# Four-layer transformer kernel: head unit 31's exponentials turned in two transfers, and new opening and order tables

## The chip, the cores and the metric

One core of a Trainium2 chip runs the whole program. Its engines have a queue of instructions each: PE (TensorE, matmuls, with its weight loads PEld), DVE (VectorE), ACT (ScalarE), POOL (GpSimd) and SP (SyncE, which here only issues DMAs). They run side by side and wait for one another by semaphores. The metric is the device time of one execution in microseconds; the number to predict is the median of several executions.

## The reference

The input is x, 1024 rows of 256. Four layers follow, each as `x = x + layernorm(f(layernorm(x)))`:

```python
qkv = (x @ w_qkv.T)                      # attention 0: 16 heads of 128, no mask
weights = softmax(q @ k.T / sqrt(128))
f0 = (weights @ v).reshape(...) @ w_out.T
hidden = silu(x @ wu.T) * (x @ wg.T)     # FFN 0: 1024 wide, ternary weights
f1 = hidden @ wd.T
scores = q_lat @ c_kv.T                  # attention 1: latent of 64, 16 heads of 16, causal
f2 = softmax(scores) @ c_kv @ v_eff
h = silu(x @ lut[gate_idx].T) * (x @ lut[up_idx].T)   # FFN 1: 688 wide, weights from a table of 16
f3 = h @ lut[down_idx].T
```

## The kernel before

**Splitting.** Products keep float32 accuracy although the operands are narrower: a value is split into an upper part (names that end in H or h) and a low part (L, l), and a product is three matmuls (lines 1000 to 1002). ACT makes the upper part from PSUM, DVE the low part.

**Stages.** `order_of_heads` (line 87) writes the order of attention 0 as a list of steps, `HEADS`. Each engine's program walks the same list and emits its own instructions of a step. FFN 0, attention 1 ("latent") and FFN 1 do the same with tables of short words (`order_of_ffn0`, `order_of_latent`, `order_of_ffn1`): a letter for the step, hexadecimal digits for its arguments. `m` is a row maximum, `w` a matmul of attention weights with its exponential, `c` the sum with the values, `u` and `h` the hidden layer of an FFN, `x` its split, `d` its down product, `s` the statistics of a layer norm, `o` and `i` its normalized outputs and inputs, `t` the transposes of the normalized input, `p` and `l` projections.

**Opening.** SP loads x in two halves and then the weights of heads 0 and 1; POOL issues the loads of two index tables (line 1946) ahead of all its work. PE runs 46 matmuls on a constant tile (`N_WARM`, line 1052). The strings `before` and `firsts` order what follows: statistics of x (`t`), normalized x (`n`), PE transposes (`T`) into XN's transposed halves xh and xl, the squares of the weights' columns (`k`, line 1381, ACT), their norm (`K`: PE, three small DVE instructions, then on POOL the scaling of both heads' weights wqr, line 1958, and q_unit, line 1966), the split of scaled weights (`Q`: wqh on ACT, wql on POOL, line 1972), and the projections `X` with their splits `x` (ACT) and `y` (DVE). `turn_in` and the projections share the two work banks 6 and 7.

**Head units.** 32 units follow, each half the queries of one head in four row blocks j. For a block: scores on PE (2 x 3 matmuls), `max` on DVE (L1661), exponential on ACT (L1423), 1/sum on DVE (L1671), normalized upper part to EP on ACT (`cast_e`, L1433), low part on DVE (`rest_e`, L1676). Then SP turns the block of EP, upper and low part together, with one transposing DMA into ET16 (L979), and `attend` (eight steps A0 to A7, three matmuls each) waits for all four blocks. `last` orders unit 31: behind the last `attend` of unit 30 stands a second run of 30 constant matmuls, then `attend` of unit 31 up to A4, the transposes of the next stage's input (`L7`), and A5 to A7.

```python
last = ("w3 i3 h3 L0 w4 l3 A7 W1 L1 L2 f0 L6 w5 L3 F0 A0 L4 A1 L5 A2 A3 A4 L7 A5 A6").split()
```

Of the kernel before, what the change touches and what calls it, by code (L numbers as in the profile page):

```python
# [30 lines left out]
N_WARM = (46, 30)  # L31
# [43 lines left out]
def f32(ap):  # L75
    return ap.bitcast(F32)
# [17 lines left out]
def order_of_heads():  # L94
# [13 lines left out]
    def project(what, *at):  # L108
# [4 lines left out]
    before = ("W0 t0 t1 n0 n1 n2 n3 k0 K0 n4 n5 n6 T0 Q0 v0 n7 T1 X0 x0 y0 Q1 X1 y1 X2 y2 x1 x2 x3 e0 v1 h0 S0 M0 "  # L113
             "v2 y3 e1 X3 x4 S1 i0 v3 M1 X4 S2 v4 e2 l0 M2 i1 i2 y4 x5 M3 S3 X5 y5 h2 l2 l1 h1 X6 X7 e3 y6 y7 "
             "x7 x6").split()
# [3 lines left out]
    for step in before:  # L119
# [7 lines left out]
        elif what == "k":  # L127
            todo.append(("square_wqk", j))
        elif what == "K":
            todo.append(("norm_wqk", j))  # L130
# [9 lines left out]
        else:  # L140
# [22 lines left out]
    weights = {(0, "w0"): [("norm_wv", 2)], (0, "w1"): [("scale_wv", 2), ("square_wqk", 2)],  # L163
               (0, "w2"): [("turn_norm", 2), ("split_wv", 2), ("norm_wqk", 2)],
# [3 lines left out]
    for u in range(NU + 1):  # L168
# [7 lines left out]
        for step in orders.get(u, order):  # L176
# [22 lines left out]
            for kind, ahead in weights.get((r, step), []):  # L199
                if h2 + ahead < H0:  # L200
                    todo.append((kind, h2 + ahead))
                    if kind in after and h2 + ahead + after[kind][1] < H0:
                        loads.append((after[kind][0], h2 + ahead + after[kind][1]))
# [70 lines left out]
def build(nc, a, out):  # L274
    with ExitStack() as top:
# [295 lines left out]
        for step in HEADS:  # L571
# [37 lines left out]
            elif what == "square_wqk":  # L609
                for i in range(4):  # L610
                    q_squared.mark(*at, i)
            elif what == "norm_wqk":
# [6 lines left out]
                for i in range(2):  # L619
                    q_back.mark(*at, i)  # L620
# [1559 lines left out]
```

## Time and profile before

| what | value |
|---|---|
| median of 3 runs | 897.76 us (896.94 to 898.62) |
| the profiled execution | 896.64 us, span 894.9 us |
| PE busy | 834.4 us, 93% of the span |
| DVE busy | 766.2 us, 86% |
| ACT busy | 607.9 us, 68% |
| POOL busy | 429.6 us, 48% |
| mean granted TensorE clock | 0.995 |

The span runs from the first to the last instruction; the execution is 1.7 us longer. The stages in time: opening 0 to about 30 us, head units to about 583, FFN 0 to about 646, latent attention to about 836, FFN 1 to the end. A timeline row gives the start, the busy time, the engine, the line, what is written and read, how many instructions it merges, and in brackets how long the engine sat idle before it and who released it.

### The profile page before, as it was taken

To read this page: it belongs to the slowest core of one execution; us is meant where nothing else is said; L and a number is where in the kernel's file an instruction comes from. 1 tells how busy PE (TensorE), PEld (TensorE's weight loads), DVE (VectorE), ACT (ScalarE), POOL (GpSimd) and SP (SyncE) were. 2 spreads that over 40 slices of the span, in tenths; PEclk is the share of its full clock that TensorE was granted. 3 is DMA by queue.
4 is the path that set the end of the run, shared out by engine and by line. 5 is a ranking of instruction groups with operands and counts; after the bars stand their busy time and mean duration, and the time that the engine had idled before them with its cause. 6 is when DMAs were issued, how large, how long until landed. Compare 5 with 4: busy or idle time off the path is not lost. (4 is left out here: it accounts for less than half of the span.)

```text
span 894.9 us, 13229 instructions
## 1 busy us (share of the span) xinstructions
PE 834.4 (93%) x4405; PEld 537.4 (60%) x4406; DVE 766.2 (86%) x1595; ACT 607.9 (68%) x1044; POOL 429.6 (48%) x456
## 2 busy tenths in 40 slices
PE   8889999999999989999998999989868999999997
PEld 3555665566566556566555666567754555554686
DVE  3788999899989999999999999766699796886647
ACT  5677767777788677776776777855565767758632
POOL 4134354444454448678679765142242354444301
PEclk9999999999999999999999999999989999999999
DMA  3487769958887677777766777630000000000001
GB/s 126 85 183 155 149 103 188 181 114 154 172 154 157 131 133 147 149 140 134 162 120 118 130 141 141 119 110 1 1 0 1 1 1 1 1 1 2 1 1 48
DMA packets 276868, 86.31 MB, mean 96 GB/s; under 512 B 267584, under 2 KB 272448, under 8 KB 276416
## 3 DMA queue, kind: packets, MB, share of 16 engines
q1 hardware_dynamic: 275520, 80.05, 45.9%
q0 software_dynamic: 992, 5.34, 2.2%
q8 instruction: 35, 0.57, 0.3%
q14 instruction: 33, 0.27, 0.1%
q10 hardware_dynamic: 288, 0.07, 0.0%
HBM read 17.29 MB, written 1.05 MB: 20 GB/s over the span
## 5 line engine op out<-in xcount | busy, mean ns | idle before, releaser
L1433 ACT ACTIVATE EP<-ps,rinv 128x1024 f16<-128x1024 f32 x128 | 142.3, 1113 | 46.7 <-DVE rinv L1671 42.9
L1676 DVE SCALAR_TENSOR_TENSOR EP<-ps,rinv,EP 128x1024 f16<-128x1024 f32 x128 | 163.3, 1276 | 3.8 <-ACT EP L1433 3.3
L1423 ACT ACTIVATE ps<-ps,nmax 128x1024 f32<-128x1024 f32 x128 | 139.2, 1088 | 34.8 <-DVE nmax L1661 34.3
L1661 DVE TENSOR_REDUCE nmax<-ps 128x1 f32<-128x1024 f32 x128 | 155.0, 1211 | 0.8 <-PE ps L1002 0.8
L1000 PE MATMUL ps<-KH,QH 128*128 128x512 f32 x256 | 115.3, 451 | 7.0 <-DVE KL L1643 4.2
L2018 POOL TENSOR_TENSOR wgu<-wgu,ptm 128x688 f32<-128x688 f32 x60 | 99.7, 1662 | 42.7 <-DVE ptm L1775 40.6
L1000 PE MATMUL ps<-ET,VH 128*128 128x512 f16 x256 | 97.2, 380 | 9.1 <-DMA ET<-EP 5.3
L2018 POOL TENSOR_TENSOR wdn<-wdn,ptm 128x512 f32<-128x512 f32 x45 | 57.7, 1283 | 92.0 <-DVE ptm L1775 90.8
L1002 PE MATMUL ps<-KH,QL 128*128 128x512 f32 x256 | 100.8, 394 | 0.0
L1001 PE MATMUL ps<-KL,QH 128*128 128x512 f32 x256 | 100.4, 392 | 0.0
L1002 PE MATMUL ps<-ET,VL 128*128 128x512 f16 x256 | 97.0, 379 | 0.0
L1001 PE MATMUL ps<-ET,VH 128*128 128x512 f16 x256 | 97.0, 379 | 0.0
L1531 ACT ACTIVATE ET<-ps 128x512 f32<-128x512 f32 (+3 forms) x144 | 60.6, 506 | 35.1 <-PE ps L1254 34.9
L1858 DVE CUSTOM_DVE_ANT_0 ps<-ps,tern 128x512 f32<-128x512 f32 (+3 forms) x128 | 72.1, 601 | 8.4 <-PE ps L1233 8.1
L1924 POOL TENSOR_TENSOR rs<-ve,mhalf 128x4 f32<-128x4 f32 (+2 forms) x22 | 19.3, 876 | 101.2 <-DVE ve L1580 78.8
L1000 PEld LDWEIGHTS ps<-KH,QH 128*128 128x128 f32 x256 | 48.2, 188 | 26.4 <-DVE EP L1676 6.9
L2080 POOL TENSOR_SCALAR_AFFINE_SELECT ET<-ET 128x128 f32<-128x128 f32 x96 | 28.4, 296 | 55.1 <-ACT ET L1531 49.6
L1002 PEld LDWEIGHTS ps<-KH,QL 128*128 128x128 f32 x256 | 48.0, 188 | 11.2
L1000 PE MATMUL ps<-xh,wqh 128*128 128x512 f16 x128 | 49.0, 383 | 4.4 <-DVE KL L1643 3.3
L1000 PEld LDWEIGHTS ps<-ET,VH 128*128 128x128 f16 x256 | 25.6, 100 | 45.2 <-DMA ET<-EP 8.6
L1001 PEld LDWEIGHTS ps<-KL,QH 128*128 128x128 f32 x256 | 48.3, 189 | 7.3
L1001 PE MATMUL ps<-xl,wqh 128*128 128x512 f16 x128 | 48.5, 379 | 0.0
(253 smaller groups left out, 2142.1 us busy)
## 6 DMA issues: line engine op xcount, KB each, us to landing
wqr<-in_wqk SPq DMA_DIRECT2D x16, 256.0 KB, 3.4
wgu<-in_tern POOLq DMA_DIRECT2D x3, 1024.0 KB, 6.7
wvr<-in_wv SPq DMA_DIRECT2D x8, 256.0 KB, 4.0
wor<-in_wo SPq DMA_DIRECT2D x16, 128.0 KB, 3.2
ET<-EP SPq DMA_TRANSPOSE x128, 4.3
X<-in_x SPq DMA_DIRECT2D x2, 512.0 KB, 5.7
prw<-in_down_idx POOLq DMA_DIRECT2D x2, 256.0 KB, 8.0
tern<-in_l_wuq_rep SPq DMA_DIRECT2D x1, 512.0 KB, 4.3
```

The source lines that it names most:

```text
L1000: e.matmul(dst, lh, rh, start=first, stop=False)
L1001: e.matmul(dst, lh, rl, start=False, stop=False)
L1002: return e.matmul(dst, ll, rh, start=False, stop=last)
L1423: e.activation(bank, bank, ACT.Exp, bias=nmax[:, c:c + 1], scale=1.0, accum_out=rsum[:, c:c + 1]).then_inc(exped.sem, 1)
L1433: e.mul(EP[:, n % NE_RING, 0, :], SB(u, j), rinv[:, c:c + 1]).then_inc(e_hi.sem, 1)
L1531: e.activation(ET[:, r, c:c + n1], ps[:, BANK[(*step, c)][0], n - n1:n], ACT.Exp).then_inc(weight_exped.sem, 1)
L1661: e.tensor_reduce(nmax[:, c:c + 1], SB(u, j), AX.X, ALU.max, negate=True).then_inc(maxed.sem, 1)
L1676: e.scalar_tensor_tensor(out=EP[:, n % NE_RING, 1, :], in0=SB(u, j), scalar=rinv[:, c:c + 1], in1=EP[:, n % NE_RING, 0, :], op0=ALU.mult, ...
L1858: e.tensor_tensor_reduce(src, src, mask[:, m0:m0 + n], 1.0, -3.0e38 if part == 0 else half, ALU.add, ALU.max, NM[:, p % 2, i8, col:col + 1 ...
L1924: e.tensor_tensor(rs[:, o, ts], ve[:, o, ts], mhalf[:, ts], ALU.pow).then_inc(ln_scale.sem, 1)
L2018: e.tensor_tensor(dst, dst, ptm[:, v % 2, 0:n], ALU.add).then_inc(lut_added.sem, 1)
L2080: e.affine_select(out=tile, in_=tile, compare_op=ALU.is_ge, fill=0.0, base=0, pattern=[[1, P]], channel_multiplier=-1).then_inc(masked.sem, 1)
```

## The change

- The last unit's `cast_e` and `rest_e` (unit 31) issue a transposing DMA each: the upper part once ACT has written it, the low part once DVE has. Both count on the block's semaphore, and `attend` waits for both. The other 31 units keep one transfer.
- Opening: x's second half is loaded behind the weights of heads 0 and 1; the two index loads become steps `I0`, `I1` further on; 24 constant matmuls instead of 46; squares, norm and scaling are done for head 0 alone and then for head 1 (`k0 K0 g0`, `k1 K1 g1`); the scaling on POOL is a step of its own (`scale_wqk`); the transposes of x go to banks 0 to 3; a new opening string.
- All three tables behind the heads are permuted: the same 83, 487 and 61 words.

```diff
-N_WARM = (46, 30)
+N_WARM = (24, 30)
...
-    before = ("W0 t0 t1 n0 n1 n2 n3 k0 K0 n4 n5 n6 T0 Q0 v0 n7 T1 X0 x0 y0 Q1 X1 y1 X2 y2 x1 x2 x3 e0 v1 h0 S0 M0 "
...
+    before = ("W0 k0 n0 t0 n1 g0 n2 Q0 K0 t1 n3 T0 v0 n5 n4 X0 n6 n7 y0 x0 T1 g1 x1 k1 x2 X1 X2 Q1 y1 K1 y2 x3 S0 "
...
     if what == "turn_in":
         for k in range(2):
-            take_work((*step, k), x_lo[at[0], k, at[1]])
+            if at[0] == 0:
+                BANK[(*step, k)] = (2 * at[1] + k, None)
+            else:
+                take_work((*step, k), x_lo[at[0], k, at[1]])
...
-            for i in range(2):
-                e.dma_start(X[:, 4 * i:4 * i + 4, :], x_v[:, 4 * i:4 * i + 4, :]).then_inc(x_in[i].sem, 16)
+            e.dma_start(X[:, 0:4, :], x_v[:, 0:4, :]).then_inc(x_in[0].sem, 16)
             for h in range(2):
                 e.dma_start(wqr[:, h, :, :], a["wqk"][:, h, :, :]).then_inc(wqk_in[h].sem, 16)
+            e.dma_start(X[:, 4:8, :], x_v[:, 4:8, :]).then_inc(x_in[1].sem, 16)
...
+                elif what == "cast_e" and at[0] == NU - 1:
+                    u, j = at
+                    w.wait_ge(*e_hi[u, j])
+                    w.wait_ge(*attended[u - 2, 7])
+                    e.dma_start(ET16[:, u % 2, 0:8, j * P:j * P + P], EP[:, (4 * u + j) % NE_RING, 0, :],
+                                transpose=True).then_inc(e_turned[(4 * u + j) % NE_RING].sem, 16)
+                elif what == "rest_e" and at[0] == NU - 1:
+                    u, j = at
+                    w.wait_ge(*e_lo[u, j])
+                    e.dma_start(ET16[:, u % 2, 8:16, j * P:j * P + P], EP[:, (4 * u + j) % NE_RING, 1, :],
+                                transpose=True).then_inc(e_turned[(4 * u + j) % NE_RING].sem, 16)
...
 # order_of_ffn0, first row of the table
-        s1044 V M h000 h010 x000 x010 o17 u020 u030 o15 h020 o16 o14 s1144 h030 x020 u040 h040 x030 i16 u050 D i15
+        s1044 V M h000 u020 h010 h020 x000 o14 o15 u030 x010 o17 o16 s1144 u040 h030 h040 x020 x030 u060 x040 i14
```

POOL at the program's start, before: rs and nb are the statistics of x, wqr the scaling of the query and key weights, wql their low part, wvs the squares of the value weights.

```order
9 L1946 DMA prw<-in_down_idx 128x512
10 L1946 DMA wgu<-in_down_idx 128x512
11 L1924 ISA
12 L1924 TENSOR_TENSOR rs<-ve,mhalf 128x4
13 L1929 TENSOR_TENSOR nb<-nm,rs 128x4
14 L1924 TENSOR_TENSOR rs<-ve,mhalf 128x4
15 L1929 TENSOR_TENSOR nb<-nm,rs 128x4
16 L1958 TENSOR_TENSOR wqr<-wqr,wfac 128x512 x2
17 L1966 TENSOR_SCALAR q_unit<-wpow 128x2 x2
18 L1972 TENSOR_TENSOR wql<-wqr,wqh 128x512
19 L1979 TENSOR_TENSOR wvs<-wvr 128x512
20 L1972 TENSOR_TENSOR wql<-wqr,wqh 128x512
```

And POOL there in the changed kernel:

```order
10 L1945 TENSOR_TENSOR rs<-ve,mhalf 128x4
11 L1950 TENSOR_TENSOR nb<-nm,rs 128x4
12 L1981 TENSOR_TENSOR wqr<-wqr,wfac 128x512
13 L1989 TENSOR_SCALAR q_unit<-wpow 128x1 x2
14 L1995 TENSOR_TENSOR wql<-wqr,wqh 128x512
15 L1945 TENSOR_TENSOR rs<-ve,mhalf 128x4
16 L1950 TENSOR_TENSOR nb<-nm,rs 128x4
17 L2002 TENSOR_TENSOR wvs<-wvr 128x512
18 L1981 TENSOR_TENSOR wqr<-wqr,wfac 128x512
19 L1989 TENSOR_SCALAR q_unit<-wpow 128x1 x2
20 L1995 TENSOR_TENSOR wql<-wqr,wqh 128x512
21 L1972 DMA prw<-in_down_idx 128x512
```

Head 0's scaling and split now stand ahead of the statistics of x's second half, and head 1's behind them.

PE at the start, in the changed kernel (before, 16 transposes stand together between the norm's matmul and the first projection, and 46 constant matmuls ahead of it):

```order
1 L1070 MATMUL ps<-filler 128x512 x24
2 L1115 MATMUL ps<-wsum,ones 128x2
3 L1030 MATMUL ps<-ident,XN 128x128 x8
4 L1018 MATMUL ps<-xh,wqh 128x512
5 L1019 MATMUL ps<-xl,wqh 128x512
6 L1020 MATMUL ps<-xh,wql 128x512
7 L1018 MATMUL ps<-xh,wqh 128x512
8 L1019 MATMUL ps<-xl,wqh 128x512
9 L1020 MATMUL ps<-xh,wql 128x512
10 L1030 MATMUL ps<-ident,XN 128x128 x8
```

The first projection, which needs only half 0 of x, has moved ahead of the second half's transposes.

DVE at the start of the latent stage, before: CS is the split latent, QH the first heads' keys, Q their queries, the ISA rows are row maxima.

```order
924 L1820 SCALAR_TENSOR_TENSOR CS<-ps,pat,R 128x512
925 L1575 BN_STATS st<-X 128x6 x2
926 L1578 BN_AGGR mv<-st 128x2 x2
927 L1580 TENSOR_SCALAR ve<-mv 128x2
928 L1586 TENSOR_SCALAR nm<-mv 128x2
929 L1596 TENSOR_TENSOR X<-X,XN 128x256 x2
930 L1840 TENSOR_TENSOR QH<-tern,R 64x512 x2
931 L1575 BN_STATS st<-X 128x6 x2
932 L1578 BN_AGGR mv<-st 128x2 x2
933 L1580 TENSOR_SCALAR ve<-mv 128x2
934 L1586 TENSOR_SCALAR nm<-mv 128x2
935 L1831 SCALAR_TENSOR_TENSOR Q<-ps,pat,R 128x512 x2
```

And in the changed kernel:

```order
926 L1605 TENSOR_SCALAR nm<-mv 128x2
927 L1841 SCALAR_TENSOR_TENSOR CS<-ps,pat,R 128x512
928 L1861 TENSOR_TENSOR QH<-tern,R 64x512 x2
929 L1615 TENSOR_TENSOR X<-X,XN 128x256 x2
930 L1852 SCALAR_TENSOR_TENSOR Q<-ps,pat,R 128x512
931 L1594 BN_STATS st<-X 128x6 x2
932 L1597 BN_AGGR mv<-st 128x2 x2
933 L1599 TENSOR_SCALAR ve<-mv 128x2
934 L1605 TENSOR_SCALAR nm<-mv 128x2
935 L1879 ISA ps,NM<-ps,tern 128x384
```

The first Q now stands ahead of the last statistics, and CS behind the statistics before it.

## Rows read from the trace of the kernel before

**Rows 1.** Busy time by stretch: start:end, length, each engine's busy time, clock, DMA.

```profile
core 0: us, PE busy (x) PEld busy (x) DVE busy (x) ACT busy (x) POOL busy (x), PEclk, DMA share, GB/s
400.00:500.00 100.00, 92.58 (x482) 59.44 (x483) 97.53 (x148) 69.38 (x106) 80.62 (x54) 1.00 0.72 132
...
590.00:626.00 36.00, 32.62 (x164) 24.51 (x163) 25.91 (x63) 21.95 (x41) 17.10 (x17) 1.00 0.21 68
...
660.00:700.00 40.00, 32.90 (x146) 20.98 (x146) 36.93 (x118) 21.78 (x39) 10.84 (x14) 0.99 0.00 1
700.00:750.00 50.00, 48.91 (x287) 29.52 (x285) 41.14 (x137) 36.25 (x82) 24.54 (x48) 1.00 0.00 1
```

**Rows 2.** Timeline of the opening, all engines: start, busy time, what.

```profile
1.39 11.93 PE L1052 MATMUL ps<-filler 128*128 128x512 bf16 x46 [1.39 <-POOL filler L1942]
...
8.29 2.07 ACT L1326 ACTIVATE XN<-X,nb,rs 128x256 f32<-128x256 f32 x4 [5.25 <-POOL nb L1929]
...
10.27 0.40 ACT L1381 ACTIVATE wsq<-wqr 128x256 f32<-128x256 f32 x1
...
10.83 1.02 POOL L1924 TENSOR_TENSOR rs<-ve,mhalf 128x4 f32<-128x4 f32 x1 [2.57 <-DVE ve L1580]
...
11.40 0.42 ACT L1381 ACTIVATE wsq<-wqr 128x256 f32<-128x256 f32 x1
...
13.15 0.28 PE L1096 MATMUL ps<-wsum,ones 128*128 128x4 f32 x2
...
14.12 2.04 POOL L1958 TENSOR_TENSOR wqr<-wqr,wfac 128x512 f32<-128x512 f32 x2 [1.99 <-DVE wfac L1703]
14.59 1.29 DVE L1604 SCALAR_TENSOR_TENSOR xl<-ps,xh 128x512 f16<-128x512 f32 x2 [0.55 <-ACT xh L1334]
...
16.76 1.16 POOL L1972 TENSOR_TENSOR wql<-wqr,wqh 128x512 f16<-128x512 f32 x1
...
18.11 0.39 PE L1000 MATMUL ps<-xh,wqh 128*128 128x512 f16 x1 [0.98 <-DVE xl L1604]
...
24.27 0.50 PE L1000 MATMUL ps<-KH,QH 128*128 128x512 f32 x1 [1.33 <-DVE KL L1643]
...
27.86 1.08 ACT L1423 ACTIVATE ps<-ps,nmax 128x1024 f32<-128x1024 f32 x1
```

**Rows 3.** DMAs: rate in 40 slices of 0:30; a load issued in 1.8:2.3, to landing.

```profile
GB/s 0 0 85 206 330 169 23 99 286 395 422 402 392 326 253 34 0 0 0 0 0 0 0 0 0 156 194 0 0 0 41 229 79 0 22 0 0 0 0 0
...
wqr<-in_wqk SPq DMA_DIRECT2D x1, 256.0 KB, 8.2
```

**Rows 4.** Timeline around the last head unit.

```profile
570.00 6.42 PE L1052 MATMUL ps<-filler 128*128 128x512 bf16 x29
577.16 0.38 PE L1000 MATMUL ps<-ET,VH 128*128 128x512 f16 x1 [0.74 <-DMA ET<-EP]
...
580.39 1.13 PE L1012 MATMUL ps<-ident,XN 128*128 128x128 f32 x8
...
578.62 2.08 ACT L1326 ACTIVATE XN<-X,nb,rs 128x256 f32<-128x256 f32 x4
```

**Rows 5.** Timeline, end of FFN 0 and start of the latent stage.

```profile
636.80 0.39 PE L1038 MATMUL ps<-KH,f0hh 128*128 128x256 f32 x1 [1.70 <-DVE XL L1607]
...
651.62 1.40 DVE L1840 TENSOR_TENSOR QH<-tern,R 64x512 fp32r<-64x512 f32 x2 [0.68 <-ACT tern L1522]
...
654.27 1.40 DVE L1831 SCALAR_TENSOR_TENSOR Q<-ps,pat,R 128x512 fp32r<-128x512 f32 x2
655.07 2.29 PE L1233 MATMUL ps<-QH,Q 128*128 128x256 f32 x7 [4.30 <-DVE Q L1831]
```

**Rows 6.** Busy time by stretch, the columns of rows 1: opening and latent start.

```profile
13.30:18.10 4.80, 2.37 (x19) 1.66 (x17) 2.53 (x7) 3.91 (x8) 3.82 (x6) 1.00 0.00 0
653.00:655.00 2.00, 0.00 (x0) 0.00 (x0) 1.90 (x9) 1.47 (x3) 1.14 (x2) 0.66 0.00 0
655.00:657.00 2.00, 1.93 (x7) 1.68 (x7) 1.99 (x9) 1.59 (x3) 1.70 (x4) 0.50 0.00 0
```

More of the change, by code:

```diff
@@ L126, in order_of_heads @@
             todo.append(("turn_in", 0, j))
[L127 to L130, printed above, removed]
+        elif what in "kKg":
+            todo.append(({"k": "square_wqk", "K": "norm_wqk", "g": "scale_wqk"}[what], j, 1))
+        elif what == "I":
+            todo.append(("load_index", j))
         elif what == "Q":
@@ L198, in order_of_heads @@
                 loads = []
-            for kind, ahead in weights.get((r, step), []):
+            for kind, ahead, *n in weights.get((r, step), []):
                 if h2 + ahead < H0:
-                    todo.append((kind, h2 + ahead))
+                    todo.append((kind, h2 + ahead, *n))
                     if kind in after and h2 + ahead + after[kind][1] < H0:
@@ L607, in build @@
                 e_lo.mark(*at)
+                if at[0] == NU - 1:
+                    e_turned[(4 * at[0] + at[1]) % NE_RING].mark(*at, "upper")
                 e_turned[(4 * at[0] + at[1]) % NE_RING].mark(*at)
             elif what == "square_wqk":
-                for i in range(4):
-                    q_squared.mark(*at, i)
+                for h in range(at[0], sum(at)):
+                    q_squared.mark(h, 0)
+                    q_squared.mark(h, 1)
             elif what == "norm_wqk":
-                q_normed.mark(*at)
-                q_norm.mark(*at)
-                q_power.mark(*at)
-                q_factor.mark(*at)
-                q_scaled.mark(*at)
-                q_scaled.mark(at[0] + 1)
+                for x in (q_normed, q_norm, q_power, q_factor):
+                    x.mark(sum(at) - 1)
+                    x.at[at[0],] = x.n
+            elif what == "scale_wqk":
+                for h in range(at[0], sum(at)):
+                    q_scaled.mark(h)
                 for i in range(2):
-                    q_back.mark(*at, i)
+                    q_back.mark(sum(at) - 1, i)
+                    q_back.at[at[0], i] = q_back.n
             elif what == "square_wv":
@@ L691, in build @@
             elif what == "norm_wqk":
-                take_work(step, q_norm[at])
+                take_work(step, q_norm[at[0]])
             elif what == "norm_wv":
@@ L1044, in _ @@
                 if what == "turn_in":
-                    turn_in(*at, WB)
+                    turn_in(*at, WB if at[0] else 0)
                 elif what == "keep_warm":
@@ L1094, in _ @@
                     w.wait_ge(*ones_in[0])
-                    w.wait_ge(*q_squared[h, 3])
-                    e.matmul(ps[:, WB + i, 0:4], f32(ones[:, :]), wsum[:, :], start=True,
+                    w.wait_ge(*q_squared[h + n - 1, 1])
+                    cs = slice(h % 2 * 2, (h % 2 + n) * 2)
+                    e.matmul(ps[:, WB + i, cs], f32(ones[:, :]), wsum[:, cs], start=True,
                              stop=True).then_inc(q_normed.sem, 1)
@@ L1406, in _ @@
                         w.wait_ge(*scored[unit_of(h - 2, (half, 1)[which]), 3])
[L1407 removed]
+                    w.wait_ge(*q_back[h, which])
                     e.mul((QH, KH)[which][:, h % 2, cs], bank, UNIT(h, which)).then_inc(qkv_hi.sem, 1)
@@ L1633, in _ @@
                 elif what == "turn_in":
-                    turn_in(*at, WB)
+                    turn_in(*at, WB if at[0] else 0)
                 elif what == "qk_lo":
@@ L1638, in _ @@
                     hi, lo = ((QH, QL), (KH, KL))[which]
-                    w.wait_ge(*q_back[h - h % 2, which])
+                    w.wait_ge(*q_back[h, which])
                     w.wait_ge(*qkv_hi[("qk", *at)])
@@ L1944, in _ @@
             e.memset(f32(ones[:, :]), 1.0).then_inc(ones_in.sem, 1)
-            for t in range(2):
-                e.dma_start(index_tile(t), TABLES[t][1]).then_inc(index_in[t].sem, 16)
             for step in HEADS:
```

127 lines of the change are left out of this document (66 added, 61 removed).

## The prediction

> **What bounds the kernel now.** I read the busy time by stretch first. Within the head units DVE is the fullest engine, 97.53 of 100 us between 400 and 500, with PE at 92.58 [rows 1]; their order is the same in both kernels, so a head unit costs what it did, and whatever the opening wins arrives, at best whole, at the end of the heads. FFN 0 leaves PE 36 - 32.62 = 3.4 us idle in 590 to 626. From 660 to 700, the start of the latent stage, DVE leads with 36.93 of 40 us and PE idles 7.1; from 700 on PE leads with 48.91 of 50 [rows 1]. So there are four places to win: the opening, the end of the last head unit, the few waits of PE in FFN 0, and the hole at the start of the latent stage. I then read the timeline at each of these.
>
> **The opening.** Today the path to the first projection (18.11) is: squares of both heads' weights from 10.27, four of them at (11.40 - 10.27) / 2 = 0.57 each; the norm's matmul at 13.15, behind the constant matmuls that end at 1.39 + 11.93 = 13.3; POOL's scaling from 14.12, 2.04 for two heads; q_unit until 16.76 (0.6); wql, 1.16, until 17.9 [rows 2]. Transposes and xl end at 14.59 + 1.29 = 15.9, so the weights are last, not x.
>
> In the changed kernel:
>
> 1. *Head 0's weights land.* Today one is issued at about 2 and lands 8.2 later, at 10.1, third in its queue behind all of x and beside POOL's two index loads. Now it is second. The first half of x (512 KB) and the identity are the 85, 206, 330 and 169 GB/s of the slices of 0.75 us from 1.5 to 4.5; the next slices that move much are 99 and 286, together 289 KB by 6.75 [rows 3]. 256 KB fit into them: I take 7.0. Bounds: not before 4.8, not after 10.1.
> 2. *Squares* of one head, 2 x 0.57: 8.2. *Constant matmuls:* 22 fewer at 6.42 / 29 = 0.22 each [rows 4] is 4.9 less: they end at 8.5. The norm's matmul goes at 8.5, and from it to POOL's scaling are 14.12 - 13.15 = 0.97: scaling 9.5 to 10.5 (one head, half of 2.04), q_unit to 11.1, wql to 12.3.
> 3. *x, half 0:* XN at 8.29, 0.52 a tile, three before the cast of the weights and the fourth behind it at about 11.1, to 11.7. Today transposes, xh and xl take from about 13.3 to 15.9, 2.6; of these only the last tile's share is left once it comes, so xl ends at about 14.0. The first projection starts at 14.1, 4.0 us earlier.
> 4. *x, half 1:* POOL's rs (1.02) and nb now stand behind wql: 12.3 to 13.6. ACT's four tiles take 2.07, to 15.7; plus 2.6 and 0.3 for the first split of K, which now stands in between: 18.6. From first projection to first score today are 24.27 - 18.11 = 6.2 for three projections with their splits; the one that is left needs about half, 3.3. First score 21.9, 2.4 earlier. The load of x's second half may land as late as 10 before it matters, since POOL is busy until 12.3.
> 5. *Head 1:* its squares follow ACT's split of Q, at about 18.4: 1.2, then 0.97, 1.02, 0.6 and 1.16 as above, with 0.5 lost between engines: wql at about 24.0. ACT's order has the split of head 1's first K ahead of the first exponential, so that one comes at about 24.0 + 1.3 + 0.9 = 26.2 instead of 27.86 [rows 2]: 1.7 earlier, and this is what the heads' pipeline takes over.
>
> The index loads, two fewer DMAs in the first 10 us, are now issued by POOL behind wql, ahead of the scaling of the value weights. POOL waits there for DVE anyway, and the tables are read only after the first unit. The banks 0 to 3 for the transposes take a wait for a bank away and no engine time. I take **-1.5** for the opening. The bounds: -4.0 (all of the first projection's lead survives) and +1.4 (the weights land at 10.1 after all: every time above moves by 3.1 and 1.7 earlier becomes 1.4 later).
>
> **The last unit's two transfers.** PE waits 0.74 us for the transfer at 577.16, but the constant matmuls, still 30, end only at 570.00 + 6.42 = 576.42 [rows 4]. However early the low part lands, A0 starts at most 0.74 earlier. Behind A4 stand the transposes, whose fourth tile comes from ACT at 578.62 + 2.08 = 580.7, and ACT's list there is the same; today they start at 580.39 and finish just behind it [rows 4]. So five of eight attends move forward and stop at a wait for ACT that was hidden until now: 0 to 0.2 is left. SP issues eight halves for four wholes; it has nothing else to do there. If a half takes as long as a whole, it is 0. I take **-0.1**.
>
> **FFN 0.** PE waits 1.70 us at 636.80 for DVE's XL, since the transposes of half 1 (t20) stand behind the last up-product (u071) and the down-products behind both [rows 5]. The new table has t20 ahead of u071, so that XH and XL are made under it. What is late next is u071's own chain (four instructions on ACT and DVE), which the down-product needs for its eighth step only. I give back 1.0 of the 1.7: **-0.7**, bounds 0 and -1.7. Of the other 3.4 us of idle PE [rows 1] most are waits for the up-products' buffers, whose DVE instructions keep their place behind the statistics: **-0.4**, bounds +1 and -2.
>
> **Start of the latent stage.** The first row-maximum matmul waits 4.30 us, until 655.07, for the first Q, which DVE makes at 654.27, behind QH (651.62, 1.40) and the last statistics [rows 5]. Now Q comes ahead of those statistics, one alone, and ACT makes the keys' halves ahead of two normalized outputs. Against it, the second CS moves behind statistics of four kinds, about 1.2 us. Counted through, QH can go at 650.1, Q ends at 653.0, and PE starts at about 653.1, 1.9 earlier. But DVE is the bound there: it idled 0.68 ahead of QH and 0.1 in 653 to 655 [rows 5, 6], and it can win only idle time. PE's clock, 0.66 in 653 to 655 and 0.50 in 655 to 657 (1.2 of 2.4 GHz) after no matmul since 650.8 [rows 5, 6], should stay at 2.4 GHz with a hole of about 1.3 us, but while DVE bounds, that buys only the second half's transposes some tenths. I take **-0.8**; bounds -4.3 (the whole wait) and +1.2 (CS's delay on the path).
>
> **The rest** of the latent table and FFN 1 are permutations of a stretch where PE is 98% full [rows 1], by which nothing can be won from 700 on but the 2% and nothing is planned to be lost: 0, bounds -2 and +5 (below).
>
> **Sum:** -1.5 - 0.1 - 0.7 - 0.4 - 0.8 = -3.5. The profiled execution took 896.64 (its span 894.9 and 1.7 around it), so 893.1; the median of the runs shown stands 1.1 above it, at 897.76, so **894.3**.
>
> **Rivals.**
>
> *The clock falls in the opening.* Between 8.8 and 14.1 PE now has only eight transposes, 1.1 us of work. Today it has 2.37 us in the 4.8 from 13.30 to 18.10, sixteen of them transposes, and the clock stays 1.00; with nothing at all it fell, from 650.8 to 655 [rows 5, 6]. The new stretch lies between. If it falls, the six matmuls of a projection take 2.6 instead of 1.3; two of them are on the path of head 1 and one more delays ACT's squares: the opening's 1.5 are gone and 0.1 more. Time 894.3 + 1.6 = 895.9. The Trainium skill ("TensorE: Matmul & The Clock Gate", Part 4: PE-mode transpose) says that transposes do not count as busy in the way matmuls do; by that rule this rival is the likely case, and before's stretch should have fallen too, where the trace shows 1.00.
>
> *More than that.* The new latent order also removes a good part of DVE's 3.1 us of idle time in 660 to 700 and of FFN 0's waits: 3.3 more, 891.0. For it, that idle time is there; against it, each wait is a chain over three engines and a permutation only moves it.
>
> *Slower:* the mechanism is in the latent stage from 700 on, where m and w steps share six PSUM banks in table order. If the new table hands PE a bank that DVE or ACT has yet to read, PE waits as it does in 660 to 700 (7.1 of 40, 18%) and not as in 700 to 750 (2%). 16% over 35 us are 5.5: 894.3 + 5.5 = 899.8. It decides from 5.3 us more of idle PE after 700. Against it, the counts of row maxima ahead of the marks of the table hardly change (38 and 39 before the first w, 148 and 148 before w80).
>
> **Chances.** Forecast 0.53, clock 0.25, more 0.15, slower 0.07. Within 0.2% (1.8 us, what a measurement of this kernel can tell from no change) is 895.96 to 899.55. Faster: 0.50 of the forecast's, 0.15, and 0.08 of the clock's: 0.73. Same: 0.03 + 0.17 + 0.01 = 0.21. Slower 0.06. The range reaches from just under the third case to the clock's case with part of the opening's other bound: 890.6 to 897.8.
>
> **What would show it.** First square at about 7.0; first projection at 14.1 and first exponential at 26.2; the granted clock 1.00 between 9 and 20. The last unit's attends start at 576.4 less the opening's gain, and the transposes behind A4 show a wait for ACT. The wait ahead of the down-products shrinks below 1 us; the first row-maximum matmul comes within 2 us of the projections, at clock 1.00. I am wrong if the first weights still land at 10, if heads' end moves by much less than the first exponential, or if PE idles more after 700.

## The result

| kernel | median us | range, runs | ratio to before, 95% interval |
|---|---|---|---|
| before | 897.39 | 896.94 to 898.62, 4 | |
| changed | 884.19 | 882.93 to 884.95, 4 | 0.9849, 0.9832 to 0.9866 |
| changed, repeated on another chip | 882.77 | 882.13 to 884.15, 5 | 0.9825, 0.9805 to 0.9844 |

The forecast was 894.3 (890.6 to 897.8), 3.5 us gained; the chip shows 13.2, and 15.6 on the other chip, where the kernel before took 898.40. One of the four executions of e14_bunched below (1043.95 us, mean granted clock 0.748) was in a slow state and is left out of its ratio, though not of its median. The profiled execution took 884.95 us, span 883.2. To see where the time went I put a few marks of each execution side by side: the starts of rows that every variant has.

| mark (us) | before | changed | difference |
|---|---|---|---|
| first exponential | 27.86 | 29.07 | +1.2 |
| OH of unit 0 | 57.61 | 57.67 | +0.1 |
| OH of unit 31, end of the heads | 583.50 | 582.53 | -1.0 |
| first R on ACT, start of the latent stage | 642.42 | 639.75 | -2.7 |
| seventh of eight reciprocals (rr), the last ahead of FFN 1; here the end of the latent stage | 819.73 | 807.93 | -11.8 |
| end of the span | 894.9 | 883.2 | -11.7 |

So 9.1 of the 11.7 us arise inside the latent stage, for which I had written -0.8 and 0.

### The profile after

**Opening.** The changed kernel's timeline, PE and ACT (start, busy time, engine, line, what, idle before), and then its busy time by stretch:

```profile
7.12 0.42 ACT L1400 ACTIVATE wsq<-wqr 128x256 f32<-128x256 f32 x1 [4.09 <-DMA wqr<-in_wqk]
...
9.12 0.28 PE L1115 MATMUL ps<-wsum,ones 128*128 128x2 f32 x2
...
12.33 0.77 PE L1030 MATMUL ps<-ident,XN 128*128 128x128 f32 x5 [1.72 <-ACT XN L1345]
14.76 0.58 PE L1018 MATMUL ps<-xh,wqh 128*128 128x512 f16 x1 [1.66 <-DVE xl L1623]
15.14 0.63 PE L1019 MATMUL ps<-xl,wqh 128*128 128x512 f16 x1
15.57 0.63 PE L1020 MATMUL ps<-xh,wql 128*128 128x512 f16 x1
...
29.07 1.08 ACT L1442 ACTIVATE ps<-ps,nmax 128x1024 f32<-128x1024 f32 x1
```

```profile
10.00:20.00 10.00, 6.45 (x24) 3.70 (x24) 4.73 (x16) 6.39 (x12) 4.84 (x7) 0.67 0.10 27
```

The weights land as forecast (7.12 for 7.0) and the first projection starts at 14.76 for 14.1, but its matmuls follow one another in 0.38 to 0.43 us, where the clock-held run below has 0.21: the granted clock over 10 to 20 us is 0.67, where 13.30 to 18.10 had 1.00 before [rows 6]. In steps of 2 us it is 0.85 in 12 to 14 and 0.50 (1.2 of 2.4 GHz) from 14 to 20, after a time in which PE did two small matmuls and eight transposes. The first exponential is at 29.07, not 26.2.

**Last unit** (changed kernel, timeline of PE and ACT):

```profile
568.35 6.64 PE L1070 MATMUL ps<-filler 128*128 128x512 bf16 x30
575.19 0.38 PE L1018 MATMUL ps<-ET,VH 128*128 128x512 f16 x1 [0.20 <-DMA ET<-EP]
...
579.30 0.33 PE L1030 MATMUL ps<-ident,XN 128*128 128x128 f32 x1 [0.16 <-ACT XN L1345]
579.79 0.76 PE L1030 MATMUL ps<-ident,XN 128*128 128x128 f32 x5 [0.16 <-ACT XN L1345]
...
577.66 2.07 ACT L1345 ACTIVATE XN<-X,nb,rs 128x256 f32<-128x256 f32 x4
```

The wait for the transfer shrinks from 0.74 to 0.20 and comes back as two waits for ACT behind A4 [rows 4], as the forecast said.

**Start of the latent stage** (changed kernel, timeline of PE, then busy time by stretch):

```profile
647.48 0.74 PE L1240 MATMUL ps<-CS,QW 128*128 128x512 f32 x2 [2.13 <-DVE CS L1841]
...
650.25 0.90 PE L1252 MATMUL ps<-QH,Q 128*128 128x384 f32 x2 [1.33 <-DVE Q L1852]
```

```profile
647.50:648.30 0.80, 0.80 (x4) 0.66 (x4) 0.77 (x2) 0.37 (x2) 0.52 (x1) 0.99 0.00 0
648.30:650.20 1.90, 0.62 (x2) 0.00 (x0) 1.87 (x5) 1.90 (x4) 0.00 (x0) 0.50 0.00 0
648.00:650.00 2.00, 0.92 (x3) 0.20 (x2) 1.94 (x5) 1.74 (x3) 0.08 (x1) 0.57 0.00 0
650.00:652.00 2.00, 1.75 (x5) 1.56 (x6) 1.93 (x10) 0.69 (x2) 0.59 (x1) 0.50 0.00 0
```

The first row maximum starts 4.8 us earlier, 2.1 of it in this stage (forecast 1.9). The clock fell to 0.5 here too, which I had not expected. It fell at about 648.3, so ahead of the hole of 1.33 us that I had looked at and behind another of 2.13: the wait for CS, which was 1.09 before and grew because CS now stands behind more statistics.

**The latent stage itself.** Its middle, 100 us long, before and then changed (columns: start:end, length, PE, PEld, DVE, ACT, POOL busy with instructions, clock, DMA share, GB/s):

```profile
700.00:800.00 100.00, 96.96 (x577) 57.75 (x576) 82.81 (x275) 69.73 (x154) 47.86 (x99) 1.00 0.00 1
```

```profile
700.00:800.00 100.00, 98.68 (x635) 60.51 (x634) 88.56 (x290) 72.98 (x161) 50.19 (x109) 1.00 0.01 1
```

PE's busy time grows by 1.8%, its matmuls in the same time by 10%. But the two windows do not hold the same work: of the 58 more matmuls 32 are short ones of the sums, 15 belong to the output and 8 to the shifts, and those of row maxima and weights are 245 before and 242 changed. The whole stage holds the same work, 911 and 912 matmuls in the traces. Here it is, before and then changed:

```profile
642.42:819.73 177.31, 160.42 (x911) 99.63 (x910) 147.75 (x477) 116.10 (x246) 76.03 (x154) 0.98 0.00 1
```

```profile
639.75:807.93 168.18, 157.50 (x912) 98.63 (x911) 147.21 (x477) 117.32 (x247) 77.26 (x153) 0.98 0.01 1
```

Of the 9.1 us that the stage is shorter, 6.2 are PE's visible idle time (16.9 to 10.7) and 2.9 lie in time shown as busy.

### The profile page after: what moved, and what is told of

Its sections match the earlier page's. It is cut to its first block, busy times and chain, and to the rows that moved or that the text cites. A ratio compares the mean times of both kernels' runs of the same rounds, so it can differ in the third digit from the quotient of the medians.

```text
span 883.2 us, 13187 instructions
## 1 busy us (share of the span) xinstructions
PE 829.2 (94%) x4386; PEld 536.2 (61%) x4386; DVE 764.3 (87%) x1598; ACT 609.4 (69%) x1044; POOL 432.5 (49%) x458
## 4 chain that ended last, share of the span: by engine, by line
PE 40%; DVE 37%; issue 8%; ACT 8%; DMA 4%; POOL 2%; DVEq 0%; ACTq 0%; POOLq 0%; SPq 0%
DVE EP L1695 10%; DVE nmax L1680 9%; PE ps L1018 6%; PE ps L1020 6%; PE ps L1019 6%; PE ps L1041 4%; DMA ET<-EP 4%; DVE ptm L1796 4%; PE ps L1056 3%; PE ps L1252 3%; PE ps L1287 3%; PE ps L1273 3%; DVE ps L1879 2%; DVE OL L1756 2%; DVE rinv L1690 1%
```

## The experiments

Ratios are to the kernel before on the same chip. Beside them stands what the profile gives without the spread of the heads: the **length of the latent stage**, from the first R to the last reciprocal ahead of FFN 1 (177.3 us before, 168.2 changed).

### One part at a time

```diff
 def order_of_latent():      # e1_latent: before, with this table from the changed kernel
 def order_of_ffn0():        # e2_ffn0: before, with this table from the changed kernel
 # e3_old_tables: changed, with all three tables put back
```

> The kernel before with one table exchanged: that of the latent stage. Theory (the gain is made where the latent table sets the order): between the last statistics before the latent stage and the start of FFN 1 the profiled executions differ by 174.6 - 166.8 = 7.8 us, and 0.6 of the 2.7 at the start belongs to it too, so 897.4 - 8.4 = about 889.0, with PE's idle time after 700 as small as in the changed kernel. Rival (the latent stage is only faster because the stage ahead of it hands over earlier or in another order): 895 to 897.5. My forecast's own step had -0.8 for this table: 896.6.

> The kernel before with one table exchanged: that of FFN 0. Theory: from the heads' end to the start of the latent stage the two profiled executions differ by 2.7 us (662.31 to 658.66, less the 0.97 that the heads bring), and all of it is this table's: 897.4 - 2.7 = 894.7. Rival (the latent stage, bound by DVE at its start, swallows it): 896.5 to 897.4. If both tables need one another, the sum of the gains of this run and of the one with the latent table alone is smaller than that of both together.

> The changed kernel with all three tables behind the heads put back: only the opening and the last unit's two transfers are new. Theory: they bring what the heads' end shows in the two profiled executions, 583.50 - 582.53 = 0.97 us or less, so 896.4 to 897.4; the first exponential comes at about 29.1 against 27.9 and the first unit ends where it did (57.6). Rival (the opening is worth the 1.5 us of my forecast and is hidden in the profile by chance): 895.9 or less.

| run | median us | ratio, 95% | latent stage |
|---|---|---|---|
| before, same chip | 899.27 | | |
| e1_latent | 889.24 | 0.9888, 0.9876 to 0.9901 | 168.2 |
| e2_ffn0 | 896.92 | 0.9971, 0.9961 to 0.9982 | 177.9 |
| e3_old_tables | 896.35 | 0.9961, 0.9948 to 0.9974 | 180.4 |

The latent table alone brings 10.0 us and gives the stage exactly the length it has in the changed kernel. FFN 0's table brings 2.4 (from the heads' end to the first R, 57.24 us for 58.92: 1.7 of them visible there), opening and last unit together 2.9, more than I expected of e3. The rival, 1.5 or more, came; at the heads' end the two profiled executions are 1.9 apart. (The old latent table took 177.3, 177.9 and 180.4 us in three profiled executions. In the last, the slowest of e3's six, the granted clock fell again in the middle, to 0.66 over 690 to 700 us where before has 1.00; PE's idle time is the same, 17.1 for 16.9. So a length of the stage is only good to some 3 us where the clock differs; the ratios do not rest on it.) The product of the three ratios is 0.9821, beside 0.9825 and 0.9849 for the changed kernel, so the parts add up within the intervals and nothing is left for FFN 1, whose table was not tried alone.

### The clock in the opening

```diff
-N_WARM = (24, 30)
+N_WARM = (24, 30, 10, 6)
-    before = ("W0 k0 n0 t0 n1 g0 n2 Q0 K0 t1 n3 T0 v0 ...
+    before = ("W0 k0 n0 t0 n1 g0 n2 Q0 K0 W2 t1 n3 T0 W3 v0 ...
```

> The changed kernel with 16 more constant matmuls in the opening's hole: 10 ahead of the transposes of x's first half and 6 behind them (nothing else moves). Theory (the fallen clock, 0.67 in 10 to 20 us, costs what the opening should have won): the granted clock stays 1.00, the first projection starts at about 14.2, the six matmuls of a projection take 1.3 instead of 2.6, the first exponential comes at 26.5 to 27.0 instead of 29.07 and the whole is 1.0 to 1.5 us below the changed kernel, 884.2 - 1.2 = 883.0. Rival (something else sets the pace of the first units, so that an earlier first exponential is lost until their end): the clock stays up, the first exponential is 2 us earlier, and the time is that of the changed kernel, 884.2.

883.45 us (880.62 to 883.66), ratio 0.9815 (0.98 to 0.9831), beside 0.9849 and 0.9825 for the changed kernel. The intervals overlap with the second, so the whole time alone does not tell the gain; the marks do. Its opening:

```profile
14.23 0.38 PE L1018 MATMUL ps<-xh,wqh 128*128 128x512 f16 x1 [0.37 <-DVE xl L1623]
14.44 0.38 PE L1019 MATMUL ps<-xl,wqh 128*128 128x512 f16 x1
...
26.24 1.08 ACT L1442 ACTIVATE ps<-ps,nmax 128x1024 f32<-128x1024 f32 x1
```

```profile
10.00:20.00 10.00, 8.46 (x45) 4.36 (x44) 6.50 (x16) 7.54 (x17) 4.43 (x7) 1.00 0.10 28
```

With the clock at 1.00 projection and exponential stand where the forecast had put them (14.1 and 26.2), and the first score too, at 21.84 for 21.9. The rival "the clock falls" is shown, and so is the rest of the opening's working. The exponential it was measured against is less firm: 27.86 is the earliest of ten profiled kernels with the old opening, whose mean is 28.39; the eight with the new one have 28.75. The Trainium skill ("TensorE: Matmul & The Clock Gate", Part 4: PE-mode transpose) has transposes not counting as matmuls do; this stretch agrees, and before's, with sixteen transposes among 2.37 us of work at 1.00 [rows 6], does not contradict it but shows that the rule alone does not say when. No run here parts the kind of work from its small amount: the matmuls that e6 adds change both.

How much of it arrives: the mean of OH's start over the ten profiled kernels with the old opening, the eight with the new one, and the two with the clock held.

| OH of unit | old | new | new, clock held |
|---|---|---|---|
| 0 | 58.10 | 57.53 | 54.95 |
| 5 | 144.23 | 143.65 | 141.03 |
| 7 | 178.42 | 176.36 | 175.25 |
| 22 | 439.24 | 437.17 | 436.08 |
| 23 | 456.59 | 453.90 | 452.68 |
| 30 | 575.88 | 573.15 | 572.09 |
| 31 | 584.65 | 581.91 | 580.85 |

Over long stretches the columns run in step to 0.02 us. They change distance at two places, behind units 6 and 22, where an engine waits for a transposing DMA. Behind unit 6 it is ACT, in before, changed and e6_warm:

```profile
162.08 1.11 ACT L1433 ACTIVATE EP<-ps,rinv 128x1024 f16<-128x1024 f32 x1 [2.03 <-DMA ET<-EP]
```

```profile
161.69 1.11 ACT L1452 ACTIVATE EP<-ps,rinv 128x1024 f16<-128x1024 f32 x1 [1.46 <-DMA ET<-EP]
```

```profile
159.95 1.11 ACT L1452 ACTIVATE EP<-ps,rinv 128x1024 f16<-128x1024 f32 x1 [2.70 <-DMA ET<-EP]
```

Behind unit 22 it is PE, 1.08 us at 448.65 before and 0.55 at 447.85 changed. There the new opening gains another 1.5 and 0.6 on average, and of the 2.6 us that the clock is worth 1.5 are lost again. POOL issues loads for the later stages shortly ahead of both places (in before at 149.27, 153.87 and 442.02), so that an earlier or later start meets them differently; that they are the cause is argued, not tried.

### One transfer in the last unit

```diff
-                elif what == "cast_e" and at[0] == NU - 1:   # upper part
-                elif what == "rest_e" and at[0] == NU - 1:   # low part
...
```

> The changed kernel once more, unaltered, as the yardstick for the other three on the same chip: 0.985 of the kernel before, as in its first runs.

> The changed kernel with one transfer per row block in the last unit, as in all others; all else as changed. My forecast gave the two transfers 0 to 0.2 us, since five of eight attends move forward and stop at the wait for ACT's fourth tile: the time is that of the changed kernel within 0.2 us. Rival (the wait for ET of 0.2 us at the first attend hides a larger one, and the first attend would come back to where it stood): 0.7 us slower.

e5: 884.65 us, 0.9843 (0.9824 to 0.9862), beside 882.77 for the changed kernel. The difference of 1.9 does not come from the last unit: from OH of unit 27 to that of unit 31 it takes 58.84 us with one transfer and 58.86 with two (the means over the old and the new opening's kernels have 58.85 and 58.86). PE's wait for the transfer is 1.26 us in e5 and 0.20 with two, and what is won there is lost to ACT at once. In the profiled executions the 1.9 are in the first exponential, 28.89 against 28.17 (kernels with this same opening spread from 28.17 to 29.15), and in the last part of the latent stage; the intervals of the two ratios overlap. The two transfers that give the change its name are worth nothing that these runs can show.

### Which engine paces the latent stage

```diff
-                    n = min(n, wide - c)
+                    n = min(n, wide - c, P)          # e9 (before), e10 (changed): row maxima on DVE
...
+                    if i8 % 2:
+                        e.matmul(ps[:, i, 0:n], QT(p)[:, i8 * P:i8 * P + P], KT[p % 4][:, hh, c:c + n],
+                                 start=True, stop=True)      # e12 (before), e13 (changed), on PE
```

> The kernel before with every row maximum of the latent stage taken over at most 128 columns on DVE (the rest of each score block is left out of the maximum): DVE's 182 instructions go from 0.60 us to about 0.33, 45 us of DVE's work less, PE's work unchanged. Theory (PE's 48.91 of 50 us busy in 700 to 750 is a matmul's modelled 0.4 us over waits for DVE of up to 0.2 us each, and DVE sets the pace in much of the stage): at least 15 us faster. Rival (PE is really full from 700 on): only the waits of the start and the 2% can go, 4 to 8 us.

> The changed kernel with the same short row maxima. Theory (the new order wins by spreading DVE's row maxima better over PE's work): with the maxima short there is less to spread, so the difference between the two tables shrinks from 10 us to 3 or less, and this is about 5 to 7 us below the kernel before with short maxima. Rival (the new order saves something on PE, ACT or POOL that has nothing to do with the maxima): the difference stays, 13 us below the kernel before with short maxima.

> The kernel before with 96 more matmuls on PE: those of the latent stage's row maxima of every second query block are done twice, back to back into the same bank. Packed, they cost 16 x (0.12 + 0.23 + 0.35 + 0.46) = 18.6 us. If PE is full from 690 on, as its busy share says, all of it comes out but what the visible waits of 8.9 us ahead of the row maxima take: 10 to 18 us slower. If much of PE's busy time is waiting inside the modelled 0.4 us of a matmul, the added work slips into it: 4 to 9 us slower.

> The changed kernel with the same 96 matmuls more. If the new order took waits, visible and hidden, out of PE's time, there are fewer left to slip into: it grows by 3 to 8 us more than the kernel before does, so that less than half of the 10 us between the two latent orders is left. If the order saves PE something else, both grow alike and the 10 us stay.

| run | median us | ratio, 95% | latent stage |
|---|---|---|---|
| e9_short_max (before) | 891.75 | 0.9919, 0.9901 to 0.9937 | 171.4 (-5.9) |
| e10_short_max_after | 877.42 | 0.976, 0.9739 to 0.9781 | 162.0 (-6.2) |
| e12_double_m (before) | 906.63 | 1.0089, 1.0073 to 1.0106 | 186.5 (+9.2) |
| e13_double_m_after | 891.45 | 0.9922, 0.9904 to 0.9939 | 176.3 (+8.1) |

The maxima's 192 instructions went from 108.0 to 58.2 us in sum, and DVE's busy time in the stage from 147.8 to 104.0. These 50 us less of DVE's work give 6; 18.6 us more of PE's cost 8 to 9, half of it. So neither engine is the bound: PE takes up half of the added matmuls. In e12 3.0 us of them went into visible idle time (16.9 to 13.9 in the stage), 9.2 made the stage longer, and the other 6.4, an estimate from the packed 18.6, went into time that was shown as busy. That time leaves almost no room to the eye, as 100 us of e12 show:

```profile
700.00:800.00 100.00, 98.39 (x603) 63.74 (x602) 80.03 (x260) 67.03 (x143) 46.17 (x90) 1.00 0.00 1
```

One part of my theory held: matmuls can slip into busy time (e12 was to cost 4 to 9 by it). Two were wrong. It expected 15 us from e9 (the rival's 4 to 8 came), and a smaller difference between the two tables in e10 and e13. It stayed: the stages are 9.4 and 10.2 us apart, the ratios 0.0159 and 0.0167, for 0.0175 between the unaltered kernels on e12's chip. So the new order's gain does not hang on the length of DVE's row maxima, and it leaves PE as much slack for added matmuls as the old one did.

### Where in the table

The first 84, or 302, of its 487 words in the new order and the rest in the old, all in the kernel before.

> The kernel before with the first 84 of the latent table's 487 words in the changed kernel's order (up to the first attention-weight step, w00) and the other 403 in the old order. The whole new table alone gave 10.0 us. Theory A (the gain is spread over the middle, where row maxima and attention weights alternate and where PE looked full): 0 to 2 us of the 10 here. Rival B (it is made at the start, where DVE bounds and PE waits 4.30 us, and is handed on): 5 or more here.

> The same with the first 302 words (up to w80, half of the heads) in the new order. Theory A: most of the 10 us, 7 to 9 here, since it holds the stretch in which the marks of the two profiled executions draw apart (reciprocal 3 at 757.67 against 747.90, reciprocal 4 at 777.52 against 765.54). Rival B: 5 to 6, hardly more than with 84 words. Rival C (the tail behind the last row maximum, with the statistics of the next stage): under 3.

e7: 896.98 us, 0.9977 (0.9962 to 0.9992), stage 175.7. e8: 890.93 us, 0.9906 (0.9884 to 0.9928), stage 170.3. Of the 9.1 us in the stage 1.6 come with the first 84 words, 5.4 with the next 218 and 2.1 with the rest: theory A. The mean granted clock over the stage is 0.98 in before, e7, e8 and e1 alike, so these lengths can be compared. The stage of e7 and then of e1, which differ behind word 84 alone:

```profile
645.11:820.77 175.66, 161.97 (x911) 99.64 (x910) 147.16 (x477) 115.86 (x246) 76.06 (x154) 0.98 0.00 1
```

```profile
642.72:810.90 168.18, 157.59 (x912) 98.69 (x911) 147.18 (x476) 117.30 (x247) 77.33 (x153) 0.98 0.00 1
```

Behind word 84, then, the new order takes away 3.1 us of visible idle time of PE (13.7 to 10.6) and 4.4 us that are shown as busy. What PE visibly waits for in 642 to 822 us, first in the kernel before, then in e1 (engine, what, line, releaser: us in total, times, longest):

```profile
PE ps L1233 <- DVE Q L1831: 6.3, 2, 4.3
PE ps L1243 <- DVE NM L1858: 2.0, 2, 1.3
PE ps L1221 <- DVE CS L1820: 1.6, 2, 1.1
PE ps L1233 <- DVE NM L1858: 0.9, 2, 0.6
```

```profile
PE ps L1221 <- DVE CS L1820: 3.1, 2, 2.1
PE ps L1233 <- DVE Q L1831: 2.2, 2, 1.2
PE ps L1279 <- ACT ET L1541: 1.7, 1, 1.7
PE ps L1243 <- DVE NM L1858: 0.6, 2, 0.3
```

Waits for Q, for the last row maxima ahead of a shift (NM) and some small ones go, the wait for CS doubles. The busy time that went with the same matmuls and the same clock must have been waiting too short to be shown; what PE waited for in it no view says.

### Row maxima against attention weights

```diff
 # words 84 to 400, only inside stretches that hold nothing but m and w words
 # e14_bunched (changed): m first, then w.   e17_w_first (changed): w first, then m.
 # e15_evened (before), e16_evened_warm (e6_warm): neighbours exchanged until the six banks' load is most even
```

> The changed kernel; in the latent table, from the first attention-weight step (word 84) to word 400, each stretch that holds only m words (a bank released by DVE, 0.33 to 0.73 us) and w words (a bank released by ACT, 0.33 to 0.57 us per matmul) is sorted: m first, then w. 39 stretches, 226 words; nothing crosses a word of another kind. Theory (the six banks go round in table order, so that six users in a row that one engine releases make PE run at that engine's pace; what the new table gains is evenness): summed over the table, a sixth of the fuller engine's work in each six neighbouring users goes from 134.3 to 150.0 us, so up to 15 us slower than the changed kernel, at least 5. Rival (the gain lies in where projections, shifts and sums stand, which stay in place here): within 2 us of the changed kernel.

> The same with w first and m behind it in each stretch. It parts bunching from delay: with m first the weights, and the sums behind them, come late; with w first they come early. By the theory of bunching both are slower alike, 134.3 to 146.8 here, 5 to 12 us; if only the delay of w costs, this one is not slower than the changed kernel.

> The kernel before with m and w words alone exchanged between neighbours inside such stretches (35 stretches) until the same sum is least: 141.4 to 131.6, where the changed kernel's table has 134.3. Theory: 4 to 10 us faster than the kernel before, with the old order of everything else. Rival: within 2 us of it.

> The changed kernel with the 16 constant matmuls that held the clock in the opening, and with its latent table evened in the same way, 134.3 to 128.2. Theory: 2 to 6 us below the one with the constant matmuls alone (0.9815 of the kernel before), so about 0.976. Rival (what bunching is left hides behind other waits): 0.9815 again.

| run | median us | ratio, 95% | latent stage |
|---|---|---|---|
| e14_bunched | 905.23 | 1.0063, 1.0048 to 1.0078 | 190.3 |
| e17_w_first | 894.66 | 0.9949, 0.9936 to 0.9963 | 180.1 |
| e15_evened | 901.18 | 1.0024, 1.0013 to 1.0036 | 180.5 |
| e16_evened_warm | 887.39 | 0.9862, 0.9849 to 0.9876 | 171.7 |

Against 168.2, bunching costs 12 us with w first and 22 with m first. The second half I put down to the delay of the weights, which no run shows by itself, and some of it is the clock's: in e14 it fell twice more, to a mean of 0.83 over 730 to 740 and over 785 to 795, and in e17 it did not. In e14 part of it shows as many small waits of the weights' matmuls (L1273) for row maxima in 700 to 800, of which neither before nor changed lists any:

```profile
PE ps L1273 <- DVE M L1879: 2.1, 10, 0.3
PE ps L1273 <- DVE NM L1879: 1.1, 5, 0.3
```

But evening out further, by my measure, made both kernels slower: by 3.2 and 3.3 us in the stage, by 2.2 and 4.2 in the ratios. The theory of evenness, as I measured it, falls: m and w can be placed badly, yet evening them is not what the old table lacked.

How much of such differences is the clock's can be estimated from the 63 executions of the kernel before on the five chips. Those with a mean granted clock of 0.990 took 900.8 us in the mean (three), 0.992 899.6 (23), 0.995 897.7 (14) and 0.998 896.0 (two): about 0.5 us for each 0.001. By that about 2 of e14's 22 us go with its clock (0.986 to 0.989, the changed kernel 0.989 to 0.994), and 1 to 3 of the 17 of x1 and x2 below (0.986 to 0.994).

### Half of the permutation each

x1 takes the places of all other words from the new table and keeps the old order of m and w; x2 the reverse, but for 51 words that had to stand up to 7 places later.

> The kernel before; in its latent table the m and w words (row maxima, attention weights) keep their old order among themselves, and all other words (projections, shifts, sums, values, statistics, normalized rows) stand at the places, counted in words, that they have in the changed kernel. Theory after the last runs (how m and w alternate is not what was won, since evening them costs 3 us and only bunching hurts; the gain lies in how far ahead of their users the projections, shifts and sums stand): 6 to 10 us faster than before, as the whole new table is (10.0). Rival (the order of the row maxima and weights among themselves carries it): 0 to 3 us.

> The other half: the m and w words in the changed kernel's order among themselves, all other words at the old places (51 of 487 words stand up to 7 places later, where a word would otherwise come ahead of what it reads). Theory of places: 0 to 3 us faster than before, or slower. Rival: 6 to 10 us faster. If both halves are near nothing, the gain needs both together: words that fit one another's places.

x1: 916.65 us, 1.0201 (1.0185 to 1.0218), stage 197.6. x2: 915.57 us, 1.0189 (1.0175 to 1.0203), stage 195.2. Both are 17 us slower than before, where the whole is 10 faster. PE's waits, x1 and then x2, 640 to 860 us:

```profile
PE ps L1268 <- POOL ET L2080: 6.9, 6, 2.0
```

```profile
PE ps L1243 <- DVE NM L1858: 8.3, 5, 2.3
```

In x1 sums stand too close behind the weights that they read, in x2 shifts too close behind their row maxima; against before these waits grew by 6.4 and 6.3 us, a third of what the stages grew by (20.2 and 17.9). Neither half carries the gain; it is in the fit of the two. Which of the many small fits is worth how much stays open.

## Why the prediction was wrong, step by step

- **The failed step** is the one on the rest: "permutations of a stretch where PE is 98% full [rows 1], by which nothing can be won from 700 on but the 2%", 0 with bounds -2 and +5, and with it -0.8 for the stage's start. Measured: 10.0 us for that table (e1), 7.5 of its 9.1 in the stage behind the first 84 words. Two things were wrong with it. The 98% is 48.91 of 50 us, read in 700 to 750 alone and carried to the whole rest, though PE still idled 3.3 us between 750 and 819.73; 3.1 of the 7.5 are such visible idle time. And I took the busy share for fullness. A matmul is shown with about 0.4 us while packed ones follow in 0.22 to 0.24, so a wait of under 0.2 us behind each leaves PE "busy": 4.4 of the 7.5 came out of busy time (e7 and e1), and e12 put an estimated 6.4 us of matmuls into it. Which words of the old order make these waits is not shown, and the cause stays open that far.
- **The rival "more than that"** pointed the right way, at DVE's idle time and FFN 0's waits, with 3.3 us for the wrong reason. The slower rival (banks handed out badly) did not happen. A table can be made bad in that way: e14 is 22 us slower in the stage, but only 3.2 us of its waits in 700 to 800 are seen to be of weights for row maxima.
- **Opening**, -1.5: the instants up to 26.24 were right with the clock held (e6), and the clock fell, as the rival had it. Its price up to unit 5 is 2.6 us. Yet opening and last unit together brought 2.9 (e3): 0.6 at unit 0, and 2.1 more on average at the two DMA waits. That the opening's gain "arrives, at best whole" was wrong, and that a gain came at all, with the clock fallen, is luck: the 1.5 was to come through a first exponential 1.7 earlier, which on average came 0.4 later.
- **Last unit**, -0.1: measured 0.0; the two waits for ACT took the place of the one for the transfer.
- **FFN 0**, -1.1: 1.7 between the marks, 2.4 as a ratio. The wait of 1.70 for XL came back as one of 1.1 ahead of another matmul, so 0.6 of it was won (forecast 0.7); the others fell from 3.5 to 2.6 (forecast 0.4). The changed kernel's list for 584 to 645:

```profile
PE ps L1041 <- DVE f0hf L1635: 1.9, 2, 1.1
PE ps L1190 <- DVE XL L1626: 1.1, 1, 1.1
PE ps L1056 <- DVE f0hl L1643: 0.5, 2, 0.3
```

- **Latent start**, -0.8: the first row maximum was forecast 1.9 earlier and came 2.1 earlier, and 1.6 us remained of the first 84 words. That the clock would stay up was wrong; it looked at the hole ahead of Q and not at the one that CS's own delay opened ahead of it.

## What to carry to other kernels

A busy share near 100% with short matmuls does not mean that the engine is full: take windows that hold the same work, and compare idle and busy time in them, or add known work and see how much of it comes out. Counting instructions in equal stretches of time misleads when the mix differs. And a share read in 50 us says nothing of the next 70. A long order of dependent words is one object; moving part of it tells nothing of the whole (+17 and +17 for halves of a -10), so a permutation of it deserves a wide range on both sides, not zero. And where an opening is made leaner, look at the granted clock in it: 16 matmuls on a constant tile gave back 2.6 us of first results, of which 1.1 arrived at the heads' end.

## What the runs showed that I had not expected

The heads keep distances to 0.02 us over 15 units and change them by 1 to 2 us at two waits for a transposing DMA; an opening's gain or loss can be doubled or eaten there. The granted clock fell to 0.5 at about 648.3 us, behind a hole of only 2.13 us and 0.8 us of matmuls, and between 12 and 14 us, with two small matmuls and eight transposes since 9.12. Where PE waited much in the middle of the latent stage it fell there too: over 700 to 800 us it is 1.00 before and changed, 0.97 in e14, 0.95 in x1 and 0.98 in x2. Half-size transposing DMAs in the last unit cost SP 1.28 to 2.03 us of issue each.
